# A GNN layer on one core: Wo's split, the third normalise and the low part of h(2) reordered in the prologue

## The chip, the cores and the metric
The kernel runs on one core of one Trainium2 chip. The metric is the device time of one execution in microseconds. The core has five engines that run their own instruction queues in order: TensorE (PE), VectorE (DVE), ScalarE (ACT), GpSimd (POOL) and SyncE (SP), which here only issues transfers. They meet at semaphores.

## The reference
`x` is (128, 64, 384), `adj` (128, 64, 64) with values 0 and 1; the weights are 384 wide.

```python
h = jnp.maximum(_layernorm(x, axis=-1), 0.0)
hi_t = h @ W1_w[:HID] (rows i) + dep_emb @ W1_w[HID:] + W1_b
hj_t = h @ W2_w[:HID] (rows j) + dep_emb @ W2_w[HID:] + W2_b
relevance = jnp.sum(hi_t * hj_t, axis=-1)
A = jax.nn.softmax(jnp.where(adj, relevance, NEG), axis=2)
aggregated = jnp.einsum('bij,bjd->bid', A, h)
h_syn = jax.nn.relu(aggregated @ gcn_w + gcn_b)
return x + h_syn @ Wo_w + Wo_b
```
The lines of hi_t and hj_t are abridged: dep_emb is the embedding of the adjacency's value.

## The kernel before
The 128 graphs are taken in 16 groups of 8, each of 512 token rows as four tiles of 128 (KT = 4, two graphs a tile). In group s the normalised tokens are h(s). W1 and W2 are folded into one matrix m, so that the scores are h m h^T plus row terms; g(s) = m applied to h, hg(s) = h times gcn_w, z(s) the attention applied to hg and passed through relu, and the output is z times Wo. Each product is made of f16 high and low parts: a high part is a rounded copy (ScalarE), a low part is the value less the high part, and three matmuls (lines 1028 to 1030) make one full product.

Everything is software pipelined by hand, the order being that in which each engine's queue is written. One TensorE iteration s does g(s) in three chunks c, then the transposes of the attention of s-1, hg(s) tile 0, the aggregation z(s-1), hg(s) tiles 1 to 3, the scores of s, and the outputs of s-1. Iterations 2 to 15 are all of this form; iteration 1 (`prev2=False`) differs, as some of the weights' preparation still lies in it: TensorE finds the peak of Wo, VectorE makes Wo's scale (`output_scale`), ScalarE the high part `wo_hi` (L587) and VectorE the low part `wo_lo` (L994, recorded as L705).

What stands around the change:
- ScalarE, iteration 1: g(1) chunks, `attention_out`, `normalise(2)` (eight instructions: for each of four tiles an f32 `h_tok` and an f16 `h_parts`), `wo_hi`, then for c = 0 to 2 `z_parts` (two instructions) and `hg_high_part`, then hg(3); after the scores of 1 it copies a part of them, runs the first half of `normalise(3)`, the exponentials of scores(1) (L611), and the second half. `normalise(s)` waits for all twenty coefficient steps of s.
- VectorE, iteration 1: g low parts, `attention_high`, `output_scale`, `statistics(3)`, `wo_lo`, then z and hg low parts, masks and sums of the scores, two output additions (L902), `attention(1)` (L939 to 951), two more additions.
- GpSimd: `token_low(2)` (one instruction, when all eight of `normalise(2)` are done), `add_bias(0)`, `main_coefficients(3)`: twenty small instructions (L340), each waiting for the one before, that make `ln_mul` and `ln_add` of x(3).
- SyncE: per group the load of a later x, the transpose of h (L261) when its low part is done, four moves of hg, and the store of an output.

TensorE's banks are shared: bank 0 holds hg tile 0 and tile 3 of the same group, so tile 3 waits (`hg_read`) until VectorE has made hg's low part of tile 0. Chunk 2 of g(s) waits until all four output additions of s-2 are done, chunk 0 of g(s) for the landed transpose of h(s).

Of the kernel before, what the change touches and what calls it, by code (L numbers as in the profile page):

```python
# [5 lines left out]
def gnn_layer_program(nc, x, adj, emb, W1, b1, W2, b2, gcn_w, gcn_b, Wo, bo, out):  # L6
# [15 lines left out]
    ALU, ACT, AX = mybir.AluOpType, mybir.ActivationFunctionType, mybir.AxisListType  # L22
# [5 lines left out]
    KT = 4  # L28
# [28 lines left out]
    with ctx:  # L57
# [51 lines left out]
        def wider(slot):  # L109
# [97 lines left out]
            w_transposed w_copied pq_projected q_copied m_done m_copied weight_peaks m_peaks  # L207
            gcn_row gcn_top gcn_wide m_row m_top m_wide type_row wo_row wo_top wo_wide wo_peak wo_scale_ready scale_step weight_scales_ready
            m_scale_ready m_high m_split gw_high gw_split gw_vector wo_high wo_split first_rows_done
            top_types top_read types_known early_t early_high early_low coef_step pairs_done pairs_copied consts_made bias_made stats_ready coef_ready h_ready h_split  # L210
            hT_landed g_done g_copied g_high g_split hg_done hg_high hg_split s_done scored
            maxed exp_bias_ready exp_done inverted att_ready attT_done attT_high z_done z_copied z_high
            z_split o_done o_added x_biased stored ty_emb_loaded ty_pe_setup ty_dve_setup ty_free ty_loaded
# [6 lines left out]
         ones_made, w_transposed, w_copied, pq_projected, q_copied, m_done, m_copied, weight_peaks, m_peaks,  # L220
         gcn_row, gcn_top, gcn_wide, m_row, m_top, m_wide, type_row, wo_row, wo_top, wo_wide, wo_peak, wo_scale_ready, scale_step, weight_scales_ready,
         m_scale_ready, m_high, m_split, gw_high, gw_split, gw_vector, wo_high, wo_split, first_rows_done,
         top_types, top_read, types_known, early_t, early_high, early_low, coef_step, pairs_done, pairs_copied, consts_made, bias_made, stats_ready, coef_ready, h_ready, h_split,
         hT_landed, g_done, g_copied, g_high, g_split, hg_done, hg_high, hg_split, s_done,
         scored, maxed, exp_bias_ready, exp_done, inverted, att_ready, attT_done, attT_high, z_done, z_copied,
         z_high, z_split, o_done, o_added, x_biased, stored, ty_emb_loaded, ty_pe_setup, ty_dve_setup, ty_free,
# [20 lines left out]
        @block.sync  # L247
        def _(sp):
            def load_x(s):
                sp.dma_start(x_all[:, s, :, :], x_rows[s, :, :, :]).then_inc(x_loaded, 16)  # L250

            def store_out(s):

                sp.wait_ge(o_added, KT * (s + 1))
                sp.dma_start(out_rows[s, :, :, :], x_all[:, s, :, :]).then_inc(stored, 16)

            def transpose_h(s, half):

                sp.wait_ge(h_split, s - 1)
                sp.wait_ge(s_done, s - 1)  # L260
                sp.dma_start_transpose(hT[half][:, :, :], h_parts[:, :, :, :].rearrange("p k n d -> p (k n d)"))\  # L261
                  .then_inc(hT_landed, 16)

            def move_hg(s):

                sp.wait_ge(hg_split, KT * (s + 1))
                if not isinstance(s, int) or s >= 1:
                    sp.wait_ge(z_done, DC * s)
                for g in range(GT):
                    rows = slice(g * S, (g + 1) * S)  # L270
                    sp.dma_start(hg_parts[0:S, :, g, :], hg_lo[rows, :, :]).then_inc(hg_moved, 16)
                    sp.dma_start(hg_parts[S:2 * S, :, g, :], hg_hi[rows, :, :]).then_inc(hg_moved, 16)

            sp.dma_start(w1_raw, W1[0:D, :].rearrange("(c p) e -> p c e", p=P)).then_inc(w1_loaded, 16)
            sp.dma_start(w1_dep[DE:DE + 1, :], b1.rearrange("(o e) -> o e", o=1)).then_inc(dep_loaded, 16)
            sp.dma_start(w2_dep[DE:DE + 1, :], b2.rearrange("(o e) -> o e", o=1)).then_inc(dep_loaded, 16)
            load_x(0)
            sp.dma_start(gcn_raw[:, :, 0:D], gcn_w.rearrange("(c p) e -> p c e", p=P)).then_inc(gcn_loaded, 16)
            sp.dma_start(gcn_raw[:, :, D:D + 1], gcn_b.rearrange("(c p o) -> p c o", p=P, o=1),
                         allow_slow_non_contiguous=True).then_inc(gcn_b_loaded, 16)  # L280

            sp.wait_ge(x_loaded, 16)
            load_x(1)
            sp.dma_start(adj_all[:, 0:HALF, :], adj_rows[:, 0:HALF, :]).then_inc(adj_loaded, 16)
            sp.dma_start(adj_all[:, HALF:, :], adj_rows[:, HALF:, :]).then_inc(adj_rest_loaded, 16)
            sp.dma_start(wo_raw[:, :, :], Wo.rearrange("(c p) e -> p c e", p=P)).then_inc(wo_loaded, 16)
            for s in range(2, 4):
                sp.wait_ge(x_loaded, 16 * s)
                load_x(s)

            with typed(sp):
                sp.dma_start(ty_emb[:, :], emb).then_inc(ty_emb_loaded, 16)
                with sp.Fori(0, NSUP) as s:

                    sp.wait_ge(ty_free, s + 1)
                    sp.dma_start(ty_x, x_rows[s, :, :, :]).then_inc(ty_loaded, 16)
                    sp.dma_start(ty_types, adj_rows[:, bass.ds(KT * s, KT), :]).then_inc(ty_loaded, 16)
                sp.wait_ge(ty_free, NSUP + 1)

            move_hg(0)  # L300
            for s in range(LAST):
                if s + 4 <= LAST:
                    sp.wait_ge(x_loaded, 16 * (s + 4))
                    load_x(s + 4)
                if s + 2 <= LAST:
                    transpose_h(s + 2, s % 2)
                move_hg(s + 1)
                store_out(s)
            for k in range(KT):

                sp.wait_ge(o_added, KT * LAST + k + 1)
                sp.dma_start(out_rows[LAST, :, k, :], x_all[:, LAST, k, :]).then_inc(stored, 16)
            sp.wait_ge(stored, 16 * (LAST + KT))
# [3 lines left out]
        def _(pool):  # L317
# [81 lines left out]
            def token_low(s):  # L399
# [2 lines left out]
                nc.gpsimd.tensor_tensor(h_parts[:, :, 1, :], h_tok[:, :, :], h_parts[:, :, 0, :],  # L402
                                        ALU.subtract).then_inc(h_split, 1)

            def add_bias(s):

                pool.wait_ge(h_ready, 2 * KT * (s + 1))
                nc.gpsimd.tensor_tensor(x_all[:, s, :, :], x_all[:, s, :, :],  # L408
                                        bo_all[:, :, :].broadcast_to([P, KT, D]),
                                        ALU.add).then_inc(x_biased, 1)  # L410
# [6 lines left out]
                    main_coefficients(s + 2)  # L417

            main_coefficients(2)
            with pool.Fori(1, LAST - 1) as s:  # L420
                iteration(s)
            iteration(LAST - 1, nxt2=False)
            iteration(LAST, nxt=False, nxt2=False)
# [4 lines left out]
        def _(act):  # L428
# [147 lines left out]
            def iteration(s, prev=True, prev2=True, nxt2=True):  # L576
                if prev:
                    for c in range(0 if prev2 else 1, DC):
                        g_high_part(s, c)
                        if c == 1 and prev2:  # L580
                            attention_out(s)
                        g_whole(c)
                    if not prev2:
                        attention_out(s)
                        normalise(2)
                        act.wait_ge(wo_scale_ready, 1)
                        nc.scalar.activation(wo_hi[:, :, :], wo_raw[:, :, :], ACT.Copy,  # L587
                                             scale=scale[:, SC_WO:SC_WO + 1]).then_inc(wo_high, 1)
                    for c in range(DC):
                        z_parts(s - 1, c, bank[Z_BANK[c]][:, :])  # L590
                        if c == 0:

                            act.wait_ge(z_done, DC * s)
                        hg_high_part(s, c)
                    hg_high_part(s, DC)
                act.wait_ge(s_done, s + 1)
                for g in range(GT):

                    if g:
                        act.wait_ge(summed, GT * s + g)  # L600
                    to, at = slice(g * S, (g + 1) * S), slice((1 - g) * S, (2 - g) * S)
                    nc.scalar.activation(score_moved[to, :, :], score_bank[at, :, g, :],
                                         ACT.Copy).then_inc(score_copied, 1)
                if nxt2 and prev:
                    normalise(s + 2, range(0, 2))
                if not prev:
                    g_high_part(1, 0)
                    g_whole(0)
                act.wait_ge(exp_bias_ready, s + 1)
                for k in range(KT):  # L610
                    nc.scalar.activation(scores[:, k, :], scores[:, k, :], ACT.Exp,  # L611
                                         bias=exp_bias[:, k:k + 1], scale=exp_scale[:, 0:1],
                                         accum_out=row_sum[:, k:k + 1]).then_inc(exp_done, 1)
                if nxt2 and prev:
                    normalise(s + 2, range(2, KT))
# [13 lines left out]
        def _(dve):  # L629
# [351 lines left out]
            def iteration(s, prev2=True, nxt2=True):  # L981
# [7 lines left out]
                if not prev2:  # L989
                    attention_high(s, prev2)  # L990
                    output_scale()
                    statistics(s + 2)
                    dve.wait_ge(wo_high, 1)
                    low_part(wo_lo[:, :, :], wo_raw[:, :, :], wo_hi[:, :, :], SC_WO).then_inc(wo_split, 1)  # L994
                for c in range(DC):
                    z_low_part(s - 1, c, bank[Z_BANK[c]][:, :])
                    rows_and_low(s, c)
                rows_and_low(s, DC)
                masked_scores(s)
                add_output(s - 1, range(2))  # L1000
# [364 lines left out]
```

## Time and profile before
| | |
|---|---|
| median of 3 runs | 378.81 us (375.56 to 379.2) |
| the profiled execution's own time | 379.19 us |
| its span, first to last instruction | 377.3 us |
| mean granted TensorE clock | 0.982 of full speed |
| PE, DVE, ACT, POOL busy | 95%, 71%, 73%, 47% |
| HBM read and written | 17.44 and 12.58 MB |

All times of the trace are microseconds from the span's start. Lines are those of the kernel before. A bracket behind an instruction gives how long its engine sat idle before it and which instruction released it.

### The profile page before, as it was taken

To read this page: it belongs to the slowest core of one execution; us is meant where nothing else is said; L and a number is where in the kernel's file an instruction comes from. 1 tells how busy PE (TensorE), PEld (TensorE's weight loads), DVE (VectorE), ACT (ScalarE), POOL (GpSimd) and SP (SyncE) were. 2 spreads that over 40 slices of the span, in tenths; PEclk is the share of its full clock that TensorE was granted. 3 is DMA by queue.
4 is the path that set the end of the run, shared out by engine and by line. 5 is a ranking of instruction groups with operands and counts; after the bars stand their busy time and mean duration, and the time that the engine had idled before them with its cause. 6 is when DMAs were issued, how large, how long until landed. Compare 5 with 4: busy or idle time off the path is not lost.

```text
span 377.3 us, 9541 instructions
## 1 busy us (share of the span) xinstructions
PE 358.4 (95%) x3154; PEld 222.8 (59%) x3154; DVE 268.2 (71%) x665; ACT 273.7 (73%) x580; POOL 178.3 (47%) x349
## 2 busy tenths in 40 slices
PE   7899883999999999999999999999999999999986
PEld 6564542656575656656565757566665656575653
DVE  1688878659686877777694958677776859576674
ACT  2375679297969788787879697887878787964733
POOL 2017506647372728274655637282836565490000
PEclk9889998799999999999999999999999999999999
DMA  8972412439564839384654646393937543434043
GB/s 237 287 246 80 108 65 50 119 104 171 151 164 130 203 83 250 84 220 114 187 126 133 156 140 175 97 236 83 250 83 199 135 127 78 132 87 147 19 123 130
DMA packets 82215, 53.87 MB, mean 143 GB/s; under 512 B 45666, under 2 KB 82148, under 8 KB 82196
## 3 DMA queue, kind: packets, MB, share of 16 engines
q1 hardware_dynamic: 81492, 52.64, 51.7%
q10 hardware_dynamic: 640, 0.79, 0.7%
q0 software_dynamic: 64, 0.20, 0.3%
q8 instruction: 11, 0.18, 0.2%
q14 instruction: 8, 0.07, 0.1%
HBM read 17.44 MB, written 12.58 MB: 80 GB/s over the span
## 4 chain that ended last, share of the span: by engine, by line
PE 87%; DVE 5%; ACT 4%; DMA 2%; issue 1%; ACTq 0%; DVEq 0%
PE bank L1028 23%; PE bank L1029 23%; PE bank L1030 23%; PE bank L1106 6%; PE bank L1260 3%; PE bank L1255 3%; PE bank L1080 2%; DMA e_col<-L_gnn_dep_emb_table_dram 2%; PE bank L1222 1%; ACT bank L611 1%; ACT h_parts L451 1%; ACT h_tok L460 1%; PE bank L1323 1%; ACT h_tok L451 1%; PE bank L1325 1%
## 5 line engine op out<-in xcount | busy, mean ns | idle before, releaser
L402 POOL TENSOR_TENSOR h_parts<-h_tok,h_parts 128x1536 f16<-128x1536 f32 x14 | 43.4, 3098 | 99.0 <-ACT h_parts L451 99.0
L1028 PE MATMUL bank<-gw_hi,hT 128*128 128x385 f16 (+2 forms) x204 | 65.2, 324 | 7.6 <-DVE hg_lo L712 6.1
L1030 PE MATMUL bank<-gw_hi,hT 128*128 128x385 f16 (+2 forms) x204 | 64.9, 323 | 0.0
L1029 PE MATMUL bank<-gw_lo,hT 128*128 128x385 f16 (+2 forms) x204 | 64.8, 322 | 0.0
L1028 PE MATMUL bank<-wo_hi,z_hi 128*128 128x384 f16 x180 | 58.7, 326 | 0.0
L1029 PE MATMUL bank<-wo_lo,z_hi 128*128 128x384 f16 x180 | 58.7, 326 | 0.0
L1030 PE MATMUL bank<-wo_hi,z_lo 128*128 128x384 f16 x180 | 58.7, 326 | 0.0
L408 POOL TENSOR_TENSOR x_all<-x_all,bo_all 128x1536 f32 (+1 forms) x16 | 56.2, 3520 | 0.0
L1028 PE MATMUL bank<-hT,m_hi 128*128 128x512 f16 x144 | 54.6, 379 | 0.0
L1030 PE MATMUL bank<-hT,m_lo 128*128 128x512 f16 x144 | 54.6, 379 | 0.0
L1029 PE MATMUL bank<-hT,m_hi 128*128 128x512 f16 x144 | 54.6, 379 | 0.0
L785 DVE TENSOR_TENSOR g_parts<-bank,g_parts 128x512 f16<-128x512 f32 x48 | 33.0, 690 | 23.9 <-ACT bank L488 23.5
L483 ACT ACTIVATE g_parts<-bank,pair_bias 128x512 f16<-128x512 f32 x48 | 32.9, 686 | 15.9 <-PE bank L1030 15.8
L451 ACT ACTIVATE h_tok<-x_all,ln_add,ln_mul 128x384 f32 (+1 forms) x56 | 39.3, 702 | 5.7 <-POOL ln_add L340 5.7
L495 ACT ACTIVATE z_hi<-bank,gcn_bias 128x512 f16<-128x512 f32 x48 | 33.7, 702 | 11.8 <-PE bank L1260 11.8
L502 ACT ACTIVATE hg_hi<-bank 128x384 f16<-128x384 f32 x64 | 32.5, 509 | 13.0 <-PE bank L1030 13.0
L451 ACT ACTIVATE h_parts<-x_all,ln_add,ln_mul 128x384 f16 (+1 forms) x56 | 39.1, 698 | 0.0
L894 DVE TENSOR_TENSOR z_lo<-bank,z_hi 128x512 f16<-128x512 f32 x48 | 32.8, 683 | 8.5 <-ACT bank L497 8.5
L902 DVE SCALAR_TENSOR_TENSOR x_all<-bank,out_scale,x_all 128x384 f32 (+1 forms) x64 | 36.4, 610 | 1.5 <-PE bank L1329 1.1
L712 DVE SCALAR_TENSOR_TENSOR hg_lo<-bank,hg_hi 128x384 f16<-128x384 f32 x64 | 35.0, 550 | 0.2 <-issue 0.2
L497 ACT ACTIVATE bank<-bank,gcn_bias 128x512 f32<-128x512 f32 x48 | 32.6, 678 | 0.0
L1028 PEld LDWEIGHTS bank<-gw_hi,hT 128*128 128x128 f16 x204 | 20.0, 99 | 21.3 <-DVE hg_lo L712 6.5
(149 smaller groups left out, 679.7 us busy)
## 6 DMA issues: line engine op xcount, KB each, us to landing
x_all<-in_x_dram SPq DMA_DIRECT2D x16, 768.0 KB, 6.4
out_dram<-x_all SPq DMA_DIRECT2D x15, 768.0 KB, 4.0
hg_parts<-hg_lo SPq DMA_DIRECT2D x32, 192.0 KB, 3.0
hg_parts<-hg_hi SPq DMA_DIRECT2D x32, 192.0 KB, 3.2
out_dram<-x_all SPq DMA_DIRECT2D x4, 192.0 KB, 1.9
x_all<-in_L_gnn_W_w_dram SPq DMA_DIRECT2D x1, 576.0 KB, 5.5
x_all<-in_L_gnn_W_w_dram ACTq DMA_DIRECT2D x1, 576.0 KB, 6.1
gcn_raw<-in_L_gnn_gcn_w_dram SPq DMA_DIRECT2D x1, 576.0 KB, 10.1
```

The lines of the kernel that those rows point to most:

```text
L402: nc.gpsimd.tensor_tensor(h_parts[:, :, 1, :], h_tok[:, :, :], h_parts[:, :, 0, :], ALU.subtract).then_inc(h_split, 1)
L408: nc.gpsimd.tensor_tensor(x_all[:, s, :, :], x_all[:, s, :, :], bo_all[:, :, :].broadcast_to([P, KT, D]), ALU.add).then_inc(x_biased, 1)
L451: nc.scalar.activation(to, x_all[:, s, k, :], ACT.Relu, bias=ln_add[:, k:k + 1], scale=ln_mul[:, k:k + 1]).then_inc(h_ready, 1)
L483: nc.scalar.activation(g_parts[:, c, :, 0, :], g_bank[c], ACT.Identity, bias=pair_bias[:, c:c + 1], scale=PROJ).then_inc(g_high, 1)
L495: nc.scalar.activation(z_hi[:, c, :], z_bank, ACT.Relu, bias=gcn_bias[:, c:c + 1], scale=Z_DOWN).then_inc(z_high, 1)
L712: nc.vector.scalar_tensor_tensor(hg_lo[:, k, :], bank[hg_banks(s)[k]][:, 0:D], PROJ, hg_hi[:, k, :], ALU.mult, ALU.subtract).then_inc(hg_s ...
L785: nc.vector.tensor_tensor(g_parts[:, c, :, 1, :], g_bank[c], g_parts[:, c, :, 0, :], ALU.subtract).then_inc(g_split, 1)
L894: nc.vector.tensor_tensor(z_lo[:, c, :], z_bank, z_hi[:, c, :], ALU.subtract).then_inc(z_split, 1)
L902: nc.vector.scalar_tensor_tensor(x_all[:, s, k, :], bank[O_BANK[k]][:, 0:D], out_scale[:, 0:1], x_all[:, s, k, :], ALU.mult, ALU.add).then ...
L1028: nc.tensor.matmul(dst, lh, rh, start=(c == 0), stop=False)
L1029: nc.tensor.matmul(dst, lh, rl, start=False, stop=False)
L1030: last = nc.tensor.matmul(dst, ll, rh, start=False, stop=(c == DC - 1))
```

## The change
It touches four queues in iteration 1 only. ScalarE: `wo_hi` directly follows `attention_out(1)`; `normalise(2)` moves behind z(0) and tiles 0 to 2 of hg(1), in front of tile 3. VectorE: `wo_lo` moves in front of `statistics(3)`, and `statistics(3)` behind the low parts of z(0) and of hg(1) tiles 0 to 2. GpSimd: the low part of h(2) is made by two instructions of two tiles each, the first when the first four instructions of `normalise(2)` are done; the loop's first iteration is written out for that. SyncE: the transpose of h(2) waits for both halves.

```diff
@@ sync, transpose_h(s, half)
                 sp.wait_ge(h_split, s - 1)
+                if s == 2:
+                    sp.wait_ge(h_half, 1)
@@ gpsimd
+            def token_low_by_halves(s):
+                half = KT // 2
+                for n, counted in ((0, h_half), (1, h_split)):
+                    pool.wait_ge(h_ready, 2 * KT * s + 2 * half * (n + 1))
+                    tiles = slice(n * half, (n + 1) * half)
+                    nc.gpsimd.tensor_tensor(h_parts[:, tiles, 1, :], h_tok[:, tiles, :], h_parts[:, tiles, 0, :],
+                                            ALU.subtract).then_inc(counted, 1)
@@
             main_coefficients(2)
-            with pool.Fori(1, LAST - 1) as s:
+            token_low_by_halves(2)
+            add_bias(0)
+            main_coefficients(3)
+            with pool.Fori(2, LAST - 1) as s:
                 iteration(s)
@@ scalar, iteration
                     if not prev2:
                         attention_out(s)
-                        normalise(2)
                         act.wait_ge(wo_scale_ready, 1)
                         nc.scalar.activation(wo_hi[:, :, :], wo_raw[:, :, :], ACT.Copy,
                                              scale=scale[:, SC_WO:SC_WO + 1]).then_inc(wo_high, 1)
@@
                         hg_high_part(s, c)
+                    if not prev2:
+                        normalise(2)
                     hg_high_part(s, DC)
@@ vector, iteration
                     output_scale()
-                    statistics(s + 2)
                     dve.wait_ge(wo_high, 1)
                     low_part(wo_lo[:, :, :], wo_raw[:, :, :], wo_hi[:, :, :], SC_WO).then_inc(wo_split, 1)
                 for c in range(DC):
                     z_low_part(s - 1, c, bank[Z_BANK[c]][:, :])
                     rows_and_low(s, c)
+                if not prev2:
+                    statistics(s + 2)
                 rows_and_low(s, DC)
```

## Rows read from the trace of the kernel before

**Rows 1.** The page's busy times: us, share of the span, instructions.
```profile
PE 358.4 (95%) x3154; PEld 222.8 (59%) x3154; DVE 268.2 (71%) x665; ACT 273.7 (73%) x580; POOL 178.3 (47%) x349
```

**Rows 2.** TensorE's waits, 57 us to the end: total us, times, longest.
```profile
PE bank L1028 <- DVE hg_lo L712: 6.1, 1, 6.1
```

**Rows 3.** Busy time of each engine in one steady iteration.
```profile
core 0: us, PE busy (x) PEld busy (x) DVE busy (x) ACT busy (x) POOL busy (x), PEclk, DMA share, GB/s
...
97.10:117.70 20.60, 20.60 (x189) 12.64 (x187) 15.15 (x37) 16.78 (x38) 11.33 (x22) 1.00 0.58 154
```

**Rows 4.** The same view around TensorE's hole; the clock is the column PEclk.
```profile
62.00:65.50 3.50, 0.00 (x0) 0.00 (x0) 3.50 (x5) 3.50 (x8) 3.50 (x2) 0.70 0.37 85
65.50:66.50 1.00, 0.95 (x4) 0.43 (x5) 1.00 (x3) 0.15 (x1) 1.00 (x1) 0.50 1.26 288
...
70.00:71.00 1.00, 1.00 (x26) 0.87 (x24) 0.66 (x5) 0.14 (x1) 0.77 (x4) 0.87 0.00 0
```

**Rows 5.** ScalarE in order of time: start us, us, engine, line, operation, operands.
```profile
55.04 0.70 ACT L451 ACTIVATE h_tok<-x_all,ln_add,ln_mul 128x384 f32<-128x384 f32 x1
...
59.23 0.70 ACT L451 ACTIVATE h_parts<-x_all,ln_add,ln_mul 128x384 f16<-128x384 f32 x1
59.83 1.25 ACT L587 ACTIVATE wo_hi<-x_all,scale 128x1152 f16<-128x1152 f32 x1
60.97 0.67 ACT L495 ACTIVATE z_hi<-bank,gcn_bias 128x512 f16<-128x512 f32 x1
...
65.13 0.51 ACT L502 ACTIVATE hg_hi<-bank 128x384 f16<-128x384 f32 x1
...
73.95 0.71 ACT L451 ACTIVATE h_tok<-x_all,ln_add,ln_mul 128x384 f32<-128x384 f32 x1 [2.25 <-POOL ln_add L340]
...
77.50 0.36 ACT L611 ACTIVATE bank<-bank,exp_bias,exp_scale 128x64 f32<-128x64 f32 x1
...
80.27 0.68 ACT L483 ACTIVATE g_parts<-bank,pair_bias 128x512 f16<-128x512 f32 x1
```

**Rows 6.** VectorE in order of time, iteration 1 into 2.
```profile
57.37 0.15 DVE L975 TENSOR_SCALAR out_half<-unscale 128x1 f32<-128x1 f32 x1
...
61.11 3.20 DVE L705 SCALAR_TENSOR_TENSOR wo_lo<-x_all,scale,wo_hi 128x1152 f16<-128x1152 f32 x1 [1.49 <-ACT wo_hi L587]
...
64.95 0.54 DVE L712 SCALAR_TENSOR_TENSOR hg_lo<-bank,hg_hi 128x384 f16<-128x384 f32 x1
...
78.02 0.18 DVE L939 RECIPROCAL row_inv<-row_sum 128x4 f32<-128x4 f32 x1 [3.61 <-ACT bank L611]
...
79.50 1.13 DVE L902 SCALAR_TENSOR_TENSOR x_all<-bank,out_scale,x_all 128x384 f32<-128x384 f32 x2
```

**Rows 7.** GpSimd in order of time, iteration 1 into 2.
```profile
60.00 3.09 POOL L402 TENSOR_TENSOR h_parts<-h_tok,h_parts 128x1536 f16<-128x1536 f32 x1 [11.66 <-ACT h_parts L451]
63.05 4.54 POOL L408 TENSOR_TENSOR x_all<-x_all,bo_all 128x1536 f32 x1
67.55 0.20 POOL L340 TENSOR_TENSOR root_sq<-stats 128x4 f32<-128x4 f32 x1
...
73.71 0.20 POOL L340 TENSOR_TENSOR ln_add<-root_sq,const_all 128x4 f32<-128x4 f32 x1
...
83.52 3.45 POOL L408 TENSOR_TENSOR x_all<-x_all,bo_all 128x1536 f32 x1
```

**Rows 8.** TensorE in order of time: a short gap, the hole's edge, iteration 2.
```profile
52.64 0.34 PE L1028 MATMUL bank<-gw_hi,hT 128*128 128x385 f16 x1 [1.15 <-DVE g_parts L785]
...
59.14 0.33 PE L1030 MATMUL bank<-gw_hi,hT 128*128 128x385 f16 x1
...
80.40 0.39 PE L1222 MATMUL bank<-ident,att_parts 128*128 128x128 f16 x4
80.69 0.39 PE L1028 MATMUL bank<-hT,m_hi 128*128 128x512 f16 x1
```

**Rows 9.** The transposes of h between 60 and 125 us.
```profile
DMA to landing us min/median/max: 4.8/7.5/8.5
```

More of the change, by code:

```diff
@@ L209, in gnn_layer_program @@
             m_scale_ready m_high m_split gw_high gw_split gw_vector wo_high wo_split first_rows_done
-            top_types top_read types_known early_t early_high early_low coef_step pairs_done pairs_copied consts_made bias_made stats_ready coef_ready h_ready h_split
+            top_types top_read types_known early_t early_high early_low coef_step pairs_done pairs_copied consts_made bias_made stats_ready coef_ready h_ready h_half h_split
             hT_landed g_done g_copied g_high g_split hg_done hg_high hg_split s_done scored
@@ L222, in gnn_layer_program @@
          m_scale_ready, m_high, m_split, gw_high, gw_split, gw_vector, wo_high, wo_split, first_rows_done,
-         top_types, top_read, types_known, early_t, early_high, early_low, coef_step, pairs_done, pairs_copied, consts_made, bias_made, stats_ready, coef_ready, h_ready, h_split,
+         top_types, top_read, types_known, early_t, early_high, early_low, coef_step, pairs_done, pairs_copied, consts_made, bias_made, stats_ready, coef_ready, h_ready, h_half, h_split,
          hT_landed, g_done, g_copied, g_high, g_split, hg_done, hg_high, hg_split, s_done,
```

## The prediction

> **What bounds the kernel now.** I began with the busy shares: TensorE is busy for 95% of a span of 377.3 us [rows 1]. A steady iteration repeats every 20.6 us and TensorE is busy in all 20.6 of them at full clock [rows 3], so whatever delays TensorE once in the prologue is never won back: no later wait is there to absorb it. Next I read who makes TensorE wait from 57 us on [rows 2]. One wait is large: 6.1 us in iteration 1, where the last hg tile waits until VectorE has split hg tile 0 and freed its bank. The windows [rows 4] show the second price of that hole: during it the granted clock falls (0.70 on average over 62 to 65.5 us), it is 0.50, the 1.2 GHz level, when the matmuls resume at 65.55, and it is back at 2.4 GHz soon after 70 us (0.87 over 70 to 71, so at about 70.25). From 65.55 to 70.25 are 4.7 us at half rate, so some 2.35 us of work are lost. The two prices together are 8.4 us.
>
> Then I followed what feeds that wait. ScalarE runs eight normalise instructions from 55.04 to 59.83 (0.60 us each), the Wo high part, and only then z and hg [rows 5]. VectorE's Wo low part starts at 61.11 and takes 3.20 us [rows 6]. The last view is what stands *behind* the third normalise, since it is what gets moved: GpSimd's low part of h(2) starts at 60.00, as the last normalise instruction ends (59.93), then comes the bias addition, then the twenty coefficient steps of h(3) [rows 7]. ScalarE's next normalise, at 73.95, is released by the last coefficient (2.25 us idle, releaser ln_add) [rows 5]. It stands in ScalarE's queue ahead of the exponentials of scores(1), which VectorE's attention waits for (3.61 us idle at 78.02) [rows 6], and that feeds TensorE's transposes at 80.40 and, through the output additions that end at 80.63, chunk 2 of g at 80.69 [rows 6, 8]. So this chain already runs within 0.1 us of TensorE before the change.
>
> **The change, step by step.**
> *ScalarE.* The scale of Wo is ready when the row of out_half ends, about 57.55 [rows 6]; nothing in the queue stands between the attention copy and it now, so the Wo high part starts at about 57.6 instead of 59.83. It takes 1.14 us to the next start (59.83 to 60.97), so z(0) starts at 58.75 instead of 60.97. The eight instructions from z(0) to the start of hg tile 2 take 4.16 us (60.97 to 65.13), and hg tile 2 some 0.37 more by the spacing that an hg eviction shows; TensorE's results for them exist by 59.5 [rows 8]. So normalise(2) starts at 63.3 instead of 55.04: **8.2 us later**. Its last instruction ends at 63.3 + 7 x 0.60 + 0.70 = 68.2 instead of 59.93. hg tile 3 starts at 68.1, against 68.67 before.
>
> *VectorE.* The low part of Wo then starts at 58.9. In the trace it overlaps GpSimd's low part; that one ends at 63.09, 1.98 us into it, and 1.22 us are left, while the bias addition behind it takes 4.54 us where a later one takes 3.45 [rows 6, 7]: the two seem to take turns. With GpSimd idle I take 1.25 us for it, with 3.20 as the upper bound. VectorE then needs the first chunk of z(0) and hg tile 0, on hand at about 60.3, and 1.2 us more (wo_lo's end at 64.31 to hg_lo's at 65.49). TensorE resumes at about 61.5 (at most 63.3) instead of 65.55. That is the intended gain: some 4 us, and since the hole shrinks to 2.1 us while the clock in the old one fell only at about 63.4 (0.70 over 3.5 us makes 2.1 us at 0.50), 3.9 us into it, perhaps the 2.35 us of low clock too. The statistics of x(3) move behind that work; they cost nothing, since VectorE otherwise waits for hg tile 3, which ScalarE starts only at 68.1, and GpSimd reads them at 73.
>
> The Trainium skill, "SBUF — State Buffer", section "Who interferes with whom", says that a VectorE instruction with two SBUF inputs and a GpSimd instruction that reads SBUF exclude each other for a whole instruction. The trace agrees: 1.98 us blocked, and the bias addition is longer by 1.09 us [rows 6, 7]. By a mere sharing of bandwidth the low part alone would take somewhere between those values; neither changes the sum below.
>
> *GpSimd.* The low part by halves: the whole takes 3.09 us, so a half about 1.55 (at most 1.8, allowing each instruction the 0.20 us that a four-element step takes) [rows 7]. The first half is covered by the remaining normalise instructions; the second starts at 68.25 and ends at **69.8**, against 63.09. Halving saves 1.55 us of a chain that starts 8.3 us later. Behind it in the same queue are the bias addition, now free of the Wo low part (3.45; at most 4.54), ending at 73.25, and the coefficients (67.55 to 73.91, 6.36, so 6.4 with the hand-over), ending at **79.6**. ScalarE's normalise(3) starts at 79.65 instead of 73.95: **+5.7 us** (5.6 to 7.0 with the two bounds). The new wait for the first half on SyncE's queue costs nothing, as the second half is later.
>
> *SyncE.* The transpose of h(2) is issued at 69.8 and lands 4.8 to 8.5 us later [rows 9], at 74.6 to 78.3. TensorE, running hg tile 3, scores (1.4 us) and outputs (5.9 us) at full clock from 61.5, is done at 70.3, so it meets a **new** wait of 4 to 8 us there. The moves of hg queue behind the transpose's issue and still have over 10 us to their reader. With two g chunks (3.9 us, up to 6.2 if the clock is low again) TensorE is ready for the attention transposes at 78.5 to 84.5.
>
> *Where it meets.* Attention is ready 5.7 us later than before, at 85.2, and the last output addition at 86.3. TensorE's chunk 2 starts at about 86.4 instead of 80.69. All that was gained at 65 us lies in front of this wait and is lost: **+5.7 us**. ScalarE's chunk 0 of g(2) moves from 80.27 to 85.97 as well, so the later work keeps its former distance from TensorE.
>
> *Clock.* TensorE has then been idle for most of 70.3 to 86.4, in a hole before the g chunks and one behind them. The nearest rows are the old hole of 6.1 us, followed by 4.7 us at 0.50 [rows 4], and a gap of 1.15 us at 51.5, after which a matmul takes 0.34 us, as at full clock [rows 8]. If the low stretch is again 4.7 us and begins with the transposes (85.25), it lasts until 89.95 and 3.55 us of it fall on work: 1.8 us lost. Bounds: 0 and 2.35. I take 1.8, as the new holes (4.3 us in front of the g chunks at the least, 0.7 to 6.7 us behind them) lie together nearer the long one. The old 2.35 us of loss is not subtracted here, because the new time at chunk 2 is built up from ScalarE's chain and not from TensorE's.
>
> Sum against the profiled execution's own time, 379.19 us (span 377.3 and 1.9 around it): 379.19 + 5.7 + 1.8 = 386.7. That execution lies 0.4 us over the median of the three runs, 378.81, so I put the median of the changed kernel at **386.3 us**. Differences under 1% (3.8 us) are about what a measurement of this kernel can't tell from none.
>
> The Trainium skill, "TensorE: Matmul & The Clock Gate", section "HAM oscillation — how this bites in real kernels", tells of gaps after which matmuls run at half rate. The trace agrees for the 6.1 us hole. By that page alone the change would look good, as it shortens this one; the chain above says that it opens two others.
>
> **Rivals.**
> *The late chain is hidden, kernel faster.* The mechanism: normalise(3) doesn't hold up attention, and only the hole at 59.5 counts. Then 4.0 and 2.35 us are saved: 378.8 − 6.3 = 372.5. It decides from the point where ln_add(3) is ready before about 73.9 and h(2) lands before 70.3. Against it: ln_add already ends a ScalarE wait in the trace, and it would have to be 5.7 us earlier than I work out. Chance 4%.
> *Only the landing counts.* Attention is in time but the transpose of h(2) isn't: chunk 0 starts at 74.6 to 78.3 instead of 76.5, so −1.9 to +1.8, near 378. Same objection; 6%.
> *No low clock after the second hole.* +5.7 alone: 384.5. For it, the gap of 1.15 us left the clock at full, and the hole behind the g chunks may be short; against it, the one in front of them is over 4 us. 18%.
> *More than one term at its upper bound*: halves at 1.8, bias addition at 4.54, low clock for the full 2.35: +7.0 + 2.35 = 388.1. The second half and the bias addition run beside VectorE's masks and sums, which could take turns with them. 12%.
> *The change doesn't do what it says*, in that ScalarE can't start Wo's high part at 57.6 but as late as before: then normalise(2) would start at 65.5, and the loss be 2.2 us bigger: 388.5. Nothing else stands ahead of it, so I count it inside the former case.
> *As worked out*, 386.3: 60%.
>
> **How the numbers follow.** The three slower cases hold 90%. Their ends, 384.5 less some 0.5 us for errors of durations and 388.1 with as much added, give 384.0 to 388.6; the start of a run scatters as well (375.56 to 379.2 before), so I widen downward to 383.2 and upward to 389.3. Faster by over 1% is 4%, within 1% 6%, slower by over 1% 90%.
>
> **What would show it.** In the changed profile: wo_hi at 57.6, normalise(2) near 63.3, wo_lo at 1.2 to 1.3 us, TensorE's wait on hg_lo down to about 2 us. If the chain is right, GpSimd's second half ends near 69.8, ScalarE idles several us before h_tok at 79.7 with releaser ln_add, TensorE waits for the transposed h(2) near 70 to 75 and again for att_parts until about 85.2, and the clock is 0.50 after it. I am wrong if coefficients or exponentials come at the old time, if GpSimd's halves cost far less than 1.5 us, or if steady iterations stop taking 20.6 us.

## The result: 2.0% slower

| | before | changed |
|---|---|---|
| median | 378.98 us (375.56 to 379.2, 4 runs) | 386.23 us (384.94 to 387.1, 4 runs) |
| ratio, first timing | | 1.0204, 95% interval 1.0146 to 1.0262 |
| ratio, timed again beside e9 | | 1.0200, 1.0164 to 1.0237 |
| span of the profiled execution | 377.3 us | 384.9 us |

That it is slower is clear; that it is slower by more than 2% isn't, as the intervals run from 1.5% to 2.6% and from 1.6% to 2.4%. The forecast was 386.3 us with a range of 383.2 to 389.3. The two executions' prologues differ by half a microsecond before the changed part is reached: the attention copy of iteration 1 starts at 54.55 us before and at 54.00 after. So events are compared below by their distance from that copy.

TensorE's waits of the changed kernel, from 57 us to the end (total us, times, longest; they answer to [rows 2]):

```profile
PE bank L1044 <- DMA hT<-h_parts: 4.3, 1, 4.3
PE bank L1238 <- DVE att_parts L966: 4.2, 2, 4.0
PE bank L1044 <- DVE hg_lo L727: 2.0, 1, 2.0
...
PE bank L1044 <- DVE x_all L917: 0.3, 1, 0.3
```

The wait that the change was aimed at fell from 6.1 to 2.0 us. Two new ones, 4.3 us for the transpose of h(2) and 4.0 us for the attention, came in its place, and one of 0.3 us for the output additions. The same in order of time, ScalarE's queue first (answers to [rows 5]; the bracket is the idle time before the instruction and its releaser):

```profile
57.01 1.26 ACT L600 ACTIVATE wo_hi<-x_all,scale 128x1152 f16<-128x1152 f32 x1 [2.42 <-DVE out_half L990]
58.17 0.67 ACT L509 ACTIVATE z_hi<-bank,gcn_bias 128x512 f16<-128x512 f32 x1
...
62.34 0.54 ACT L516 ACTIVATE hg_hi<-bank 128x384 f16<-128x384 f32 x1
62.71 0.77 ACT L465 ACTIVATE h_tok<-x_all,ln_add,ln_mul 128x384 f32<-128x384 f32 x1
...
66.89 0.73 ACT L465 ACTIVATE h_parts<-x_all,ln_add,ln_mul 128x384 f16<-128x384 f32 x1
...
79.04 0.71 ACT L465 ACTIVATE h_tok<-x_all,ln_add,ln_mul 128x384 f32<-128x384 f32 x1 [5.01 <-POOL ln_add L342]
...
82.59 0.36 ACT L626 ACTIVATE bank<-bank,exp_bias,exp_scale 128x64 f32<-128x64 f32 x1
...
85.37 0.69 ACT L497 ACTIVATE g_parts<-bank,pair_bias 128x512 f16<-128x512 f32 x1
```

normalise(2) runs from 62.71 instead of 55.04. ScalarE then idles 5.01 us before normalise(3), and the releaser is ln_add, GpSimd's last coefficient. GpSimd (answers to [rows 7]; its coefficient steps have line 342 here, 340 before):

```profile
65.33 1.65 POOL L413 TENSOR_TENSOR h_parts<-h_tok,h_parts 128x768 f16<-128x768 f32 x1 [17.51 <-ACT h_parts L465]
67.70 1.64 POOL L413 TENSOR_TENSOR h_parts<-h_tok,h_parts 128x768 f16<-128x768 f32 x1 [0.73 <-ACT h_parts L465]
69.30 3.42 POOL L419 TENSOR_TENSOR x_all<-x_all,bo_all 128x1536 f32<-128x1536 f32 x1
72.67 0.21 POOL L342 TENSOR_TENSOR root_sq<-stats 128x4 f32<-128x4 f32 x1
...
78.81 0.20 POOL L342 TENSOR_TENSOR ln_add<-root_sq,const_all 128x4 f32<-128x4 f32 x1
```

These are the links of the chain: second half of h(2)'s low part until 69.34, bias addition until 72.72, twenty coefficient steps until 79.01, ScalarE at 79.04. VectorE and TensorE at its far end (answer to [rows 6, 8]):

```profile
58.30 1.42 DVE L720 SCALAR_TENSOR_TENSOR wo_lo<-x_all,scale,wo_hi 128x1152 f16<-128x1152 f32 x1 [1.07 <-ACT wo_hi L600]
...
60.36 0.55 DVE L727 SCALAR_TENSOR_TENSOR hg_lo<-bank,hg_hi 128x384 f16<-128x384 f32 x1
...
68.64 4.46 DVE L930 TENSOR_SCALAR masks<-adj_all,row_term 128x64 f32<-128x64 f32 x4
73.20 0.90 DVE L940 TENSOR_TENSOR bank<-bank,masks 64x256 f32<-64x256 f32 x2
...
83.12 0.18 DVE L954 RECIPROCAL row_inv<-row_sum 128x4 f32<-128x4 f32 x1 [6.78 <-ACT bank L626]
...
84.59 1.13 DVE L917 SCALAR_TENSOR_TENSOR x_all<-bank,out_scale,x_all 128x384 f32<-128x384 f32 x2
```

```profile
60.97 0.34 PE L1044 MATMUL bank<-gw_hi,hT 128*128 128x385 f16 x1 [2.05 <-DVE hg_lo L727]
...
74.15 0.61 PE L1044 MATMUL bank<-hT,m_hi 128*128 128x512 f16 x1 [4.28 <-DMA hT<-h_parts]
...
84.93 0.58 PE L1238 MATMUL bank<-ident,att_parts 128*128 128x128 f16 x4 [3.97 <-DVE att_parts L966]
85.78 0.61 PE L1044 MATMUL bank<-hT,m_hi 128*128 128x512 f16 x1 [0.27 <-DVE x_all L917]
```

The last output additions end at 85.72, chunk 2 of g(2) starts at 85.78. That is 31.78 us behind the attention copy; before it was 80.69 − 54.55 = 26.14. The difference, **5.64 us**, is the first term of the loss. The second is in the windows (answers to [rows 4]; the granted clock is the number behind the busy times, here followed by DMA share and GB/s):

```profile
65.00:70.00 5.00, 4.87 (x30) 2.73 (x28) 2.59 (x6) 3.39 (x7) 3.94 (x3) 1.00 0.00 0
...
74.00:75.00 1.00, 0.85 (x3) 0.31 (x4) 0.93 (x3) 0.03 (x1) 0.84 (x3) 0.50 0.86 204
...
80.00:82.00 2.00, 0.96 (x5) 0.23 (x3) 0.00 (x0) 2.00 (x6) 0.00 (x0) 1.00 0.00 0
82.00:84.00 2.00, 0.00 (x0) 0.00 (x0) 0.81 (x3) 2.00 (x8) 0.00 (x0) 0.79 0.00 0
...
88.30:89.30 1.00, 1.00 (x4) 0.43 (x3) 0.80 (x2) 0.00 (x0) 1.00 (x2) 0.50 0.92 217
89.30:90.30 1.00, 1.00 (x6) 0.42 (x5) 0.00 (x0) 0.46 (x1) 1.00 (x1) 0.65 1.08 346
...
105.00:125.60 20.60, 20.60 (x189) 12.67 (x188) 15.18 (x38) 16.52 (x37) 11.36 (x22) 1.00 0.57 154
```

The clock falls in the hole in front of the g chunks, is at 0.50 through most of them, recovers after 79 us, falls again in the second hole and stays at 0.50 until about 90.0 (0.65 over 89.3 to 90.3). From 85.78 to 90.0 are 4.2 us of work at half rate: **2.1 us** lost. Then the steady iterations run as before, 20.60 busy us in 20.60 [rows 3]. 5.6 + 2.1 = 7.7 us. From the attention copy to the end of the span the changed kernel needs 330.9 us, the one before 322.75: 8.15 us more, so some 0.4 us lie elsewhere. They lie behind chunk 2: from its start to the end of the span are 299.1 us, against 296.6 before, which is 2.5 and not 2.1. What makes them is open.

### The profile page after: what moved, and what is told of

Same layout as the page of the kernel before. It is cut to its first block, busy times and chain, and to the rows that moved or that the text cites. A ratio compares the mean times of both kernels' runs of the same rounds, so it can differ in the third digit from the quotient of the medians.

```text
span 384.9 us, 9517 instructions
## 1 busy us (share of the span) xinstructions
PE 360.8 (94%) x3154; PEld 222.2 (58%) x3154; DVE 270.5 (70%) x665; ACT 273.8 (71%) x580; POOL 178.0 (46%) x350
## 4 chain that ended last, share of the span: by engine, by line
PE 82%; ACT 6%; DVE 5%; POOL 3%; DMA 2%; issue 2%; ACTq 0%; DVEq 0%; POOLq 0%
PE bank L1044 22%; PE bank L1045 22%; PE bank L1046 22%; PE bank L1122 5%; PE bank L1276 3%; PE bank L1271 3%; DMA e_col<-L_gnn_dep_emb_table_dram 2%; PE bank L1096 2%; ACT bank L626 1%; ACT h_tok L465 1%; ACT h_parts L465 1%; PE bank L1238 1%; POOL x_all L419 1%; DVE x_all L917 1%; ACT h_tok L474 1%
## 5 line engine op out<-in xcount | busy, mean ns | idle before, releaser
L404 POOL TENSOR_TENSOR h_parts<-h_tok,h_parts 128x1536 f16<-128x1536 f32 x13 | 40.3, 3100 | 87.5 <-ACT h_parts L465 87.5
L1044 PE MATMUL bank<-hT,m_hi 128*128 128x512 f16 x144 | 56.6, 393 | 4.5 <-DMA hT<-h_parts 4.3
L1045 PE MATMUL bank<-hT,m_hi 128*128 128x512 f16 x144 | 56.4, 392 | 0.0
L1046 PE MATMUL bank<-hT,m_lo 128*128 128x512 f16 x144 | 56.4, 391 | 0.0
L419 POOL TENSOR_TENSOR x_all<-x_all,bo_all 128x1536 f32 (+1 forms) x16 | 55.1, 3452 | 0.0
L617 ACT ACTIVATE score_moved<-bank 64x256 f32<-64x256 f32 x32 | 12.1, 379 | 31.2 <-DVE bank L940 17.4
```

The source lines that it names most:

```text
L1044: nc.tensor.matmul(dst, lh, rh, start=(c == 0), stop=False)
L1045: nc.tensor.matmul(dst, lh, rl, start=False, stop=False)
L1046: last = nc.tensor.matmul(dst, ll, rh, start=False, stop=(c == DC - 1))
```

## The experiments

Each of the kernels e1 to e10 was timed beside the kernel before in five rounds; the ratio is to that. "Chunk 2" is its start behind the attention copy of iteration 1 in the run's trace, "normalise(3)" the start of its first instruction counted in the same way.

| run | median us | ratio (95%) | normalise(3) | chunk 2 |
|---|---|---|---|---|
| before | 378.6 to 379.3 | 1 | 19.40 | 26.14 |
| changed | 386.23 | 1.0204 (1.0146 to 1.0262) | 25.04 | 31.78 |
| e10, changed again | 386.97 | 1.0200 (1.0164 to 1.0237) | 25.04 | 31.79 |
| e9, ScalarE's part alone | 388.36 | 1.0246 (1.0210 to 1.0281) | 26.45 | 33.19 |
| e2, changed, low part whole | 387.81 | 1.0236 (1.0195 to 1.0277) | 26.45 | 33.19 |
| e5, changed, holes filled | 384.46 | 1.0133 (1.0096 to 1.0169) | 25.01 | 31.98 |
| e4, changed, exponentials first | 384.98 | 1.0159 (1.0123 to 1.0196) | 25.04 | 25.95 |
| e6, changed, own coefficients | 381.88 | 1.0067 (1.0042 to 1.0092) | 21.46 | 28.20 |
| e3, changed, coefficients first | 380.81 | 1.0066 (1.0042 to 1.0089) | 21.61 | 28.71 |
| e8, changed, ScalarE undone | 380.67 | 1.0038 (1.0015 to 1.0061) | 20.27 | 27.01 |
| e1, halves alone | 377.08 | 0.9976 (0.9954 to 0.9998) | 17.97 | 24.71 |
| e7, interleaved | 375.70 | 0.9902 (0.9874 to 0.9929) | 17.28 | 21.93 |

> The changed kernel once more, beside the run of ScalarE's order alone, for a common chip: 386.2, ratio 1.02, if nothing but the scatter of the first timing stood behind its wide interval.

The second timing of the changed kernel agrees with the first, in time and, to 0.01 us, in the place of normalise(3) and of chunk 2.

Theory A is the prediction's: normalise(2) moved back delays GpSimd's low part, bias and coefficients(3), hence normalise(3), hence everything queued behind it on ScalarE. Rival B says that only TensorE's own holes, the landing of h(2) and the clock count. Rival C blames the sums of scores(1).

**Which part does it: e9 and e8.** e9 takes the kernel before and moves ScalarE's instructions alone:

```diff
                         attention_out(s)
-                        normalise(2)
                         act.wait_ge(wo_scale_ready, 1)
...
                         hg_high_part(s, c)
+                    if not prev2:
+                        normalise(2)
                     hg_high_part(s, DC)
```


> The kernel before with ScalarE's order alone changed (Wo's high part, z(0) and hg tiles 0 to 2 ahead of normalise(2)); VectorE and GpSimd as before. Theory A: statistics(3) stand in front of Wo's low part, so TensorE's first hole ends some 0.7 us later than in the changed kernel, which lies in front of the wait for h(2) and costs nothing; the low part of h(2) is whole, so everything from it on is 1.4 us later than in the changed kernel, as in the run with the whole low part: 387.7. Rival B (TensorE's holes): 0.7 more, 388.4. If ScalarE's move is not the cause but VectorE's or GpSimd's part is, the time is that of the kernel before.

Measured 388.36, 0.7 over the forecast and next to B's 388.4; the times do not part A from B here, but the trace does: TensorE's first hole is 2.7 us instead of 2.0, as both said, and chunk 2 starts at 33.19, exactly where e2 has it, so those 0.7 us didn't reach chunk 2. ScalarE's move alone makes a loss (2.1 to 2.8%) as large as that of the whole change, or larger. e8 is its complement, the changed kernel with this move taken back:

> The changed kernel with ScalarE's order alone put back; VectorE's and GpSimd's parts stay. Theory A: normalise(2) ends at the old time, the second half at 61.7; Wo's low part runs 1.4 us earlier than before; but statistics(3) now stand behind it and end at 68.3, which makes coefficients(3) begin at 68.3 instead of 67.6: normalise(3) 0.8 us later than before and the kernel at 379.4, against 386.2 for the whole change. Rival B (landing and clock): the hole at Wo is 1.4 us shorter and h(2) lands 1.4 us earlier, so 376 to 377.5.

Measured 380.67, 1.3 over A's forecast and 3 over the top of B's. normalise(3) is 0.87 us later than before, as worked out from statistics(3). The rest fits a price that I hadn't put in: this opens a hole of 2.2 us before the transposes, after which the clock was at 0.50 from about 81.5 to 85 us in the profiled execution. That execution took 381.97 us, 1.3 over the median; whether the others (378.75 to 382.52) paid the same wasn't looked at. VectorE's moved statistics, which the prediction booked at nothing, do cost the 0.87 us as soon as ScalarE's move no longer covers them: GpSimd idles 2.34 us for them.

```profile
68.35 0.20 POOL L342 TENSOR_TENSOR root_sq<-stats 128x4 f32<-128x4 f32 x1 [2.34 <-DVE stats L651]
...
80.57 0.38 PE L1237 MATMUL bank<-ident,att_parts 128*128 128x128 f16 x4 [2.19 <-DVE att_parts L965]
```

**What the halves are worth: e2 and e1.** e2 puts one `token_low(2)` back into the changed kernel:

```diff
-            token_low_by_halves(2)
+            token_low(2)
```


> The changed kernel with the low part of h(2) as one instruction again. Theory A: the low part ends at 70.8 instead of 69.3, and bias, coefficients(3), normalise(3), attention and chunk 2 of g(2) all follow 1.4 us later: 387.6, 1.4 us over the changed kernel. Rival B (the landing of h(2) and the clock): the landing is 1.4 us later too, so also some 1.4 us; this run sizes the halves only and does not part the two.

normalise(3) moved from 25.04 to 26.45: 1.41 us. The median is 1.6 us over the first timing of the changed kernel and 0.8 over the second; the intervals overlap, so the trace's 1.41 us is the firmer number. e1 puts the halves alone into the kernel before:

> The kernel before with one part of the change alone, the low part of h(2) by halves. Theory A (the new time is set by GpSimd's chain low part of h(2), bias, coefficients(3), which holds normalise(3) and with it the exponentials of scores(1)): the second half ends about 1.4 us earlier than the whole did, so Wo's low part is blocked 1.4 us less, TensorE's hole ends near 64.1 instead of 65.55, normalise(3) starts at about 72.7 instead of 73.95 and the kernel gains 1.2 us, 377.7. Rival B (only TensorE's own holes and the landing of h(2) count): a gain of 1.4 us by the shorter hole, and up to 2.3 more if the clock then stays high. A says that the latter is not collected at chunk 2 of g(2), as attention is not ready.

A gain of 0.9 us (0.1 to 1.7) was measured, with 1.43 us at normalise(3) and at chunk 2; so this one part of the change is good by itself. The clock still fell in the first hole of 4.6 us (0.50 over 60 to 66 us), so B's further gain wasn't there to collect. In its trace Wo's low part takes 1.75 us instead of 3.20:

```profile
59.31 1.75 DVE L719 SCALAR_TENSOR_TENSOR wo_lo<-x_all,scale,wo_hi 128x1152 f16<-128x1152 f32 x1 [1.48 <-ACT wo_hi L601]
```

```profile
58.22 1.64 POOL L413 TENSOR_TENSOR h_parts<-h_tok,h_parts 128x768 f16<-128x768 f32 x1 [0.74 <-ACT h_parts L465]
59.81 4.54 POOL L419 TENSOR_TENSOR x_all<-x_all,bo_all 128x1536 f32<-128x1536 f32 x1
```

It starts 0.55 us before GpSimd's second half ends (59.86), and the bias addition behind it takes 4.54 us again, in place of 3.42 when no Wo low part is near.

**Is it the coefficients: e3.** One line moves on GpSimd, nothing in front of the landing of h(2) changes:

```diff
             token_low_by_halves(2)
-            add_bias(0)
             main_coefficients(3)
+            add_bias(0)
```


> The changed kernel with GpSimd's coefficients(3) ahead of the bias addition of group 0; landing of h(2) and everything up to there unchanged. Theory A: normalise(3) starts 3.4 us earlier (75.7 instead of 79.04), the exponentials end at 79.7, the output additions that wait for the bias (now done at 79.1) end at 80.2 and delay attention a little, so chunk 2 of g(2) starts at about 82.9 instead of 85.78: a gain of 2.9 us. The second hole of TensorE is then only some 1.5 us, the clock stays high behind it, and 1.9 us more are gained: 381.5. Rival B (landing of h(2) and its low clock set the time): nothing before the landing changes, so 386.2.

```profile
PE bank L1044 <- DMA hT<-h_parts: 4.3, 1, 4.3
PE bank L1238 <- DVE att_parts L966: 2.2, 2, 1.9
```

380.81 against 381.5 forecast; B's 386.2 is out. TensorE's wait for h(2) is unchanged at 4.3 us, the one for attention fell to 1.9 us, and the clock is 1.00 from 79 us on. This is the run that decides for A against B. Against C it says nothing, since moving the bias addition frees the masks of scores(1) too (1.24 us instead of 4.46); e4 parts those two.

**Is it because normalise(3) stands in front of the exponentials: e4.**

```diff
-                if nxt2 and prev:
+                if nxt2 and prev and prev2:
                     normalise(s + 2, range(0, 2))
...
                 if nxt2 and prev:
-                    normalise(s + 2, range(2, KT))
+                    normalise(s + 2, range(2, KT) if prev2 else range(KT))
```


> The changed kernel with ScalarE's whole normalise(3) behind the exponentials of scores(1). Theory A: the exponentials no longer wait for coefficients(3); they run at 75.3, attention is ready at 78.4 before TensorE has ended its two g chunks at 80.3, and chunk 2 of g(2) starts at about 80.6 instead of 85.78. But normalise(3) still starts at 79.04 and now all eight instructions stand in front of the evictions of g(2), which start at 83.85 instead of 85.4, so hg tile 0 of group 2 starts at about 85.8 instead of 89.6: a gain of 3.8 us, 382.5, and TensorE's wait moves from att_parts to g_parts. Rival B (landing and clock): no gain, 386.2. Rival C (attention is late because the masks and sums of scores(1) are blocked by GpSimd's bias addition until 72.7, not because of the coefficients): the exponentials would still end at 83, no gain.

```profile
76.11 0.38 ACT L626 ACTIVATE bank<-bank,exp_bias,exp_scale 128x64 f32<-128x64 f32 x1 [1.29 <-DVE exp_bias L949]
```

```profile
PE bank L1044 <- DVE g_parts L800: 3.8, 1, 3.8
PE bank L1044 <- DMA hT<-h_parts: 2.7, 1, 2.7
```

Chunk 2 came 5.83 us earlier, at 25.95, earlier even than before the change, and the wait on att_parts is down to 0.3 us. C falls: with the masks as late as in the changed kernel (4.46 us), the exponentials start at 76.11, 21.3 us behind the attention copy, in place of 27.45; it was 21.8 before the change. But as expected the wait reappears as one for g_parts, 3.8 us: normalise(3) still starts at 25.04, and g(2)'s evictions stand behind it. The total was 2.5 us worse than my 382.5, and its interval overlaps the changed kernel's, so the trace and not the time speaks here. I had left out that the clock would fall once more in this hole: it was at 0.50 from the restart at 86.61 until about 89.5, which is some 1.4 of the 2.5 us. The rest is open. To let the exponentials pass is worth little while the coefficients are late.

**Does the landing matter once the coefficients are in time: e6.** The coefficients of h(3) get tiles of their own and are made while GpSimd idles, ahead of the halves; VectorE's statistics(3) go back in front of Wo's low part. The cut shows GpSimd's lines:

```diff
+            pool.wait_ge(stats_ready, 4)
+            coefficients(3, stats6, ln3_mul, ln3_add, coef_ready)
             token_low_by_halves(2)
             add_bias(0)
-            main_coefficients(3)
```


> The changed kernel with the coefficients of h(3) in tiles of their own, made while GpSimd is idle and ahead of the low part of h(2); VectorE's statistics(3) back in front of Wo's low part, so that they are in time. Theory A with its second limit: without the late coefficients ScalarE's normalise(3) waits only for the landing of h(2) (74.1), the exponentials end at 78.1, chunk 2 of g(2) starts at about 80.9 instead of 85.8, and there is one hole less, so that the clock is high behind it: 6.5 to 7 us gained, 379.4, about the time of the kernel before. The 8 us gained at Wo are then still lost, to the landing of h(2). Rival (the coefficients were the whole cause, the landing is no limit): 373 to 375, as TensorE would have kept all it gained at Wo.

```profile
PE bank L1047 <- DMA hT<-h_parts: 3.3, 1, 3.3
```

```profile
76.18 0.71 ACT L469 ACTIVATE h_tok<-x_all,ln_add,ln_mul 128x384 f32<-128x384 f32 x1 [1.01 <-DMA hT<-h_parts]
```

381.88: clearly above the rival's 373 to 375, and normalise(3) is now released by the landing of h(2), so this is a second limit behind the first. It isn't alone: ScalarE idled for it only 1.01 us, as its copy of the scores in front of it waited until 74.79 for the sums behind the masks, which took 4.87 us beside GpSimd. An earlier landing alone would thus have moved normalise(3) by about 1 us. The run also misses my 379.4. Chunk 2 lies at 28.20, while 26.9 was forecast: the transpose was issued 0.4 us later, as the coefficients ended at 67.28 and held up the first half, and it took 5.6 us to land, in place of 4.7 in the changed kernel, with the moves of hg behind it in both. Why the landing was slower is not settled.

**The clock's share: e5.** Spare matmuls keep TensorE busy in both new holes:

```diff
+            def fill(b, count):
+                for _ in range(count):
+                    nc.tensor.matmul(bank[b][:, 0:D], gw_hi[:, 0, 0:P], gw_hi[:, 0, 0:D], start=True, stop=True)
...
+                        if isinstance(s, int) and s == 2:
+                            fill(1, 25)
...
+                            fill(6, 40)
                         transposed_attention()
```


> The changed kernel with spare matmuls (their results are overwritten) in TensorE's two new holes: 25 in front of chunk 0 of g(2) and 40 in front of the attention transposes of iteration 2; iterations 2 and 3 of TensorE's loop are written out for it. Theory A: the start of chunk 2 of g(2) is set by ScalarE and VectorE, so it stays 31.8 us behind the attention copy of iteration 1, and what is gained is the low clock behind it alone, 1.9 us (the changed kernel was at 0.50 until 89.9, 4.1 us behind chunk 2's start): 384.3. Rival (the clock costs nothing on the path, the whole difference is waiting): 386.2. Rival B (TensorE's own clock in front of chunk 2 matters too): more than 3 us gained.

```profile
61.00:66.00 5.00, 4.32 (x52) 3.22 (x53) 4.70 (x13) 5.00 (x11) 0.00 (x0) 0.66 0.00 0
...
74.00:78.00 4.00, 4.00 (x23) 2.13 (x22) 2.91 (x7) 0.38 (x1) 3.14 (x12) 1.00 0.82 207
78.00:82.00 4.00, 4.00 (x23) 2.13 (x22) 0.00 (x0) 2.28 (x4) 1.22 (x7) 1.00 0.02 5
...
86.00:90.00 4.00, 4.00 (x26) 2.21 (x25) 2.35 (x5) 4.00 (x8) 3.77 (x2) 1.00 0.66 208
```

384.46 against 384.3. Chunk 2 hardly moved (31.98), the clock behind it is 1.00, and from it to the end of the span this trace needs 2.1 us less than the changed kernel's (297.0 against 299.1). The median is 1.8 us under the first timing of the changed kernel and 2.5 under the second. So the clock is worth some 2 us, and the chain the remaining 5 to 5.6.

**A version that beats both: e7.** ScalarE uses its idle time until Wo's scale is there for half of normalise(2), and does the other half behind z(0)'s first chunk and hg tile 0; normalise(3) stands behind the exponentials, coefficients(3) ahead of the bias, all output additions behind the attention. The cut shows ScalarE's lines up to hg:

```diff
                         attention_out(s)
+                        normalise(2, range(0, 2))
                         act.wait_ge(wo_scale_ready, 1)
...
                         hg_high_part(s, c)
-                    if not prev2:
-                        normalise(2)
+                        if c == 0 and not prev2:
+                            normalise(2, range(2, KT))
                     hg_high_part(s, DC)
```


> A kernel built on theory A, to beat both: ScalarE does half of normalise(2) while Wo's scale is made, then Wo's high part, the first chunk of z(0) and hg tile 0, the other half of normalise(2), the rest; normalise(3) wholly behind the exponentials of scores(1); GpSimd's low part by halves, then coefficients(3), then the bias; VectorE's statistics(3) behind hg tile 0 and all four output additions behind attention(1). Theory A: h(2) is split at 63.9 and landed at 68.7, before TensorE needs it at 71.3; chunk 2 of g(2) starts about 21.9 us behind the attention copy of iteration 1 (before: 26.1; changed: 31.8): 4.2 us faster than before, 374.6. Rival (every microsecond saved at Wo comes back as a later wait, whatever the order): 378 to 379.

375.70 us, ratio 0.9902, which is 3.7 us of the forecast 4.2. Chunk 2 starts at 21.93, as worked out (21.9).

```profile
PE bank L1046 <- DVE hg_lo L728: 2.3, 1, 2.3
...
PE bank L1240 <- DVE att_parts L967: 0.3, 1, 0.3
```

Neither the landing nor the attention makes TensorE wait any more. The first hole is still 2.3 us and was followed by low clock here (0.50 over 61 to 64 us). As several things were changed at once, the run shows that the order can be made faster, and not what each of them is worth.

## Why the prediction was right

- *ScalarE's move delays normalise(2) by 8.2 us*: it starts 8.71 us behind the attention copy, 0.49 before, so 8.2. Right, and e9 shows that this alone makes the loss.
- *Wo's low part alone takes 1.25 us*: it took 1.42, a little over the 1.2 to 1.3 that were to be seen. So of the 3.20 us before, 1.78 were blocked and not 1.98. TensorE's hole ended at 60.97, 4.0 us earlier by distance from the copy, as forecast.
- *A half takes 1.55 us*: 1.65 and 1.64, so a half costs 0.1 us more than half of the whole's 3.09. Within the bound of 1.8.
- *Bias addition 3.45, coefficients 6.4*: 3.42 and 6.34, from 72.67 to 79.01.
- *normalise(3) 5.7 us later, and with it chunk 2*: 5.64 for both.
- *The landing is a new wait of 4 to 8 us that costs nothing by itself*: 4.3, and 2.7 in e10, where low clock behind the first hole made TensorE later; covered in both. e6 shows that it becomes a limit when the coefficients are in time.
- *Two g chunks take 3.9 us, up to 6.2 at low clock*: they ran from 74.15 to 80.96, 6.8 us, as the clock stayed at 0.50 until about 79.8. The bound was too tight; it cost nothing, since TensorE then still waited 3.97 us for the attention.
- *Low clock behind chunk 2, 1.8 us*: 2.1 in this trace. In e10 the clock fell later (0.90 over 84 to 86 us) and was back earlier, at 89; there 1.45 us were lost. e5 confirms the term by taking it away. Whole, the part behind chunk 2 is 2.5 us in the trace; 0.4 of it no term of the prediction covers.
- *The statistics of x(3) cost nothing*: right in the changed kernel, but only as ScalarE's move hides them; see e8.
- *What was not forecast*: the masks of scores(1). They took 4.46 us instead of 0.73, as they couldn't get past the second half and the bias addition; the prediction has this only as a risk in a rival. It cost nothing, since exp_bias was ready at 75.3 and the exponentials waited for ScalarE until 81.45. In e3, where the bias addition isn't next to them, they took 1.24.

The mechanism was right, link by link. That 386.23 lies within 0.1 us of the forecast is luck: by distance from the attention copy the changed execution lost 8.15 us and not 7.5, and it made good 0.55 us by a faster start, before the changed part. Timed again, the same kernel has a median of 386.97.

The rival in which the chain is hidden needed ln_add before 73.9; it came at 79.0.

## What to carry to other kernels

Before moving a producer back in an engine's queue, follow what it releases to its last reader, through the other engines' queues and in their order: here eight instructions of ScalarE held up three pieces of work on GpSimd (low part, bias addition, coefficients), and these held up ScalarE itself one stage later. An engine that is 47% busy, as GpSimd was, can be the limit of a stage. A hole that is filled early in such a kernel is worth only what the next wait allows, so look for the next one first; and idle time in the queue that is to be relieved (2.4 us before Wo's high part) is the place for half of the moved work.

## What the runs showed of the hardware

VectorE's masks, four tensor_scalar instructions from SBUF to SBUF with 64 elements a partition each, took 0.73 us beside four-element steps of GpSimd (iteration 1 before the change), and 4.46 and 5.91 us (e2) when GpSimd's tensor_tensor on 768 to 1536 elements a partition ran beside it; each time they were done 0.4 us after the end of the bias addition. VectorE's low parts of g, which read one operand from PSUM, kept their 0.69 us beside GpSimd's low part and bias addition (at 81.52 and 83.34 us in the trace of before). The Trainium skill, "SBUF — State Buffer", section "Who interferes with whom", lists tensor_scalar among the operations that can take the pair of ports which VectorE shares with GpSimd, if its operands meet certain conditions. The 4.46 and 5.91 us agree with that. It went the other way round too: in e6 GpSimd's first coefficient step, on four elements, took 1.30 us instead of 0.20 beside Wo's low part on VectorE, which started 0.16 us before it:

```profile
59.87 1.30 POOL L344 TENSOR_TENSOR root_sq<-stats 128x4 f32<-128x4 f32 x1 [11.45 <-DVE stats L656]
```

The clock after a short hole isn't a constant of the kernel. Six traces have the same hole of 2.0 us in front of hg tile 3. Behind it the changed kernel, e2 and e3 kept 1.00; e4, e5 and e10, which is the changed kernel's code, fell to 0.50. In e10 that was over 62 to 64 us:

```profile
60.00:62.00 2.00, 0.71 (x4) 0.46 (x5) 1.95 (x6) 2.00 (x5) 0.00 (x0) 0.93 0.00 0
62.00:64.00 2.00, 2.00 (x11) 0.97 (x10) 1.74 (x5) 2.00 (x5) 0.00 (x0) 0.50 0.00 0
64.00:66.00 2.00, 2.00 (x50) 1.94 (x48) 1.95 (x5) 2.00 (x4) 0.36 (x1) 0.72 0.00 0
```

In the changed kernel that is covered by the later wait. In e7, where TensorE is the limit from there on, it is not. It doesn't explain the scatter of e7's executions (374.12 to 376.0), though: the profiled one, with low clock behind that hole, is the fastest of the six. What makes the scatter is open.
